# The order of one step's front work on TensorE: head sums and key norms last

## The chip, the core and the metric

The kernel runs on one NeuronCore of one Trainium2 chip, as a single launch. The metric is the device time of the launch in microseconds (us). The profile's engines are TensorE (PE, with its weight loads as PEld), VectorE (DVE), ScalarE (ACT), GpSimd (POOL) and SyncE (SP), which issues most of the DMAs. TensorE writes only to PSUM, which has eight banks of 128 partitions by 512 float32 numbers. One matmul result of this kernel fits in one bank.

## The reference, cut to what matters

The input is x, of shape (4, 1024, 128). The layer first normalises each row, and then runs a linear-attention recurrence with 16 heads of 8 channels each:

```
q, k, v = silu(x @ Wq), silu(x @ Wk), silu(x @ Wv)
f       = sigmoid(x @ Wf1 @ Wf2)                 # exp(log_sigmoid)
gamma   = -sigmoid(x @ Wg)                       # one per head
k       = k / max(norm(k per head), 1e-12)
a       = k * gamma
S1 = S + a (k . S);  S2 = f * S1;  S3 = S2 + a (k . S2) + k v;  o = q . S3
out3 = stack([0, 0, o]) ... out = out3[:, -N:]   # every third row carries an o
```

The result is gated, normalised again, projected with Wout and added to x. After it comes a mixture of experts: a router chooses one of 16 experts for each token, and a shared expert runs beside them. Only the o of the last third of the recurrence reaches the output, and in the output every third row (here called "mixed") has an attention part. The other two thirds (called "others") do not, so their part of the router can be worked out early.

## The kernel before, in words

**Tiling.** The 1024 tokens of each sequence are cut into 32 chunks (C = 32), so that 4 x 32 = 128 chunks lie on the partitions. The recurrence over time becomes the product of per-token 8 x 8 matrices. Each chunk builds the product of its own matrices and a running sum of its v terms, walking backward through its tokens. These are the backward loops. There are NT = 32 steps: steps 0 to 20 walk the first 21 slots of each chunk (L1 = 21), and steps 21 to 31 walk the last 11 (L2 = 11). After them a chain on VectorE joins the chunks, a forward loop follows, and then come the gate, the projection and the experts.

**One step of the backward loops.** It works on two halves h of the state, half 1 first, and each half lives in PSUM banks 2h and 2h + 1. `grow` (line 1531) multiplies the state by three factors in one VectorE instruction. TensorE's `sums(h, i)` (lines 1952 and 1953) adds over heads: line 1952 gives what `u_term` (line 1553) needs, and line 1953 gives what `y_term` (line 1559) needs. `next_state` (line 1565) adds the terms and waits for GpSimd's `add_u_term` (line 1131). VectorE's order in loop pass i is: u_term and y_term of half 1, u_term of half 0, next state of half 1, y_term of half 0, grow of half 1 for step i, next state of half 0, grow of half 0, and then `front(i)`. ScalarE's `ucopy` (line 926), GpSimd's `v_times_u` (line 1045) and TensorE's `add_sum` (line 1962) gather the v terms.

**The front work.** Each step also carries some preparation for later steps. A group of 3 or 4 slots is transposed (kind `xT`, line 1745), projected (`K`, `V`, `Q`, `G`, `F`, line 1757), its key norms are worked out (`squares`, line 1765; `rk`, line 1774), and a head sum is formed (`c`, line 1779). Work for the gate (`xaT`, line 1796; `gate`, line 1802), for the router of the "others" rows (`rowsT`, line 1810; `logits`, line 1820; `ranks` and `totals`, line 1828) and the transposes of two weights (`ffn_w`, line 1786) is spread over the steps too. The function `uses(i)` lists the items of step i. It is the one source of their order, and all four engines walk that list.

**Banks.** All front items share banks 6 and 7. `ports()` deals the banks out strictly by turns: item number k over all steps gets bank 6 + k % 2. TensorE's `port(kind, n)` waits until the item before on the same bank has been taken, and then fills the bank. ScalarE takes most items: `evict` (line 776), `evict_slot` (line 783), and line 846 for `totals`. VectorE takes two kinds: `rk` in `keys` (line 1468) and `c` in `c_keys` (line 1475). VectorE does this in its `front(i)`, which walks `uses(i - 1)`, the list of the step before, and stands behind both grow instructions of step i. The same `front` runs the router's parts from step 22 on: part 4, in step 26, is the scan at line 1310, and it first waits until `totals` has been taken.

**TensorE's order** in step i is sums of half 1 and half 0 (each waits for its grow), add_sum of both halves for step i - 1, and then `front(i)`. Its queue is in order, so a front item that waits holds back the sums of step i + 1. GpSimd's `y_keys` feeds `c`; it runs in the same step, and its next call waits until the `c` before has been filled. No engine writes an order by cost: all of it is written out by hand.

Of the kernel before, what the change touches and what calls it, by code (L numbers as in the profile page):

```python
# [127 lines left out]

def uses(i):

    found = []
    if i == 0:
        found += [("K", 2), ("V", 2)]
    if i == 1:
        found += [("G", 2), ("F", 2)]
    for n in range(EARLY, NG):
        ahead = NEED[n] - i
        if ahead == 8:
            found.append(("xT", n))
        if ahead == 7:  # L140
            found += [("K", n), ("V", n)]
            if GROUPS[n][0] >= L1:
                found.append(("Q", n))
        if ahead == 6:
            found += [("G", n), ("F", n)]
    for n in range(2, NG):
        ahead = NEED[n] - i
        if ahead == 5:
            found.append(("squares", n))
        if ahead == 4:  # L150
            found.append(("rk", n))
        if ahead == 2:
            found.append(("c", n))
    if i in (2, 3):
        found.append(("ffn_w", i - 2))
    for g in range(NQ):
        if i == 8 + 4 * g:
            found.append(("xaT", g))
        if i == 11 + 4 * g:
            found.append(("gate", g))  # L160
    for g in range(len(OTHERS.groups)):
        if i == 9 + 2 * g:
            found.append(("rowsT", g))
        if i == 10 + 2 * g:
            found.append(("logits", g))
    if i == 25:
        found += [("ranks", 0), ("totals", 0)]
    return found


FIRST = [("xT", 0, 0), ("K", 0, 2), ("low", 0, 7), ("xT", 1, 1), ("K", 1, 3), ("wfo", 0, 7), ("squares", 0, 6),
# [4 lines left out]
def ports():  # L176

    count, at = [0] * 8, {}

    def put(kind, n, b):  # L180
        at[kind, n] = (b, count[b])
        count[b] += 1

    for kind, n, b in FIRST:
        put(kind, n, b)
    first = list(count)
    for k, (kind, n) in enumerate(u for i in range(NT) for u in uses(i)):
        put(kind, n, 6 + k % 2)
    return at, first, count
# [9 lines left out]
def build(nc, a, out, xs, ys, scr):  # L199

    ctx = ExitStack()
    with ctx:
# [526 lines left out]
        def _(act):  # L729
# [76 lines left out]
            def front(i):  # L806

                for kind, n in uses(i):
                    if kind == "xT":
                        evict(kind, n, xnT[n % 2][:, 0:wide_of(n)], cols=wide_of(n))  # L810
# [105 lines left out]
            for i in range(NT):  # L916
                for kind, n in uses(i):
                    if kind == "rk":
                        spread_rk(n)
                if i == L1:  # L920
                    copy_sums(b_out.rearrange("p (a b) -> p a b", a=2))
                for h in (1, 0):

                    act.wait_ge(s_uterm[h], i + 1)
                    act.wait_ge(s_bp[h], i + 1)
                    S.activation(ucopy[:, h], bank[2 * h + 1], ACT.Copy).then_inc(s_uc[h], 1)  # L926
                front(i)
# [1236 lines left out]
```

## Time and profile before

| what | value |
|---|---|
| median of 3 runs | 642.89 us (642.54 to 643.53) |
| profiled execution | 641.85 us, its span 639.7 us, mean granted clock 0.947 |
| PE busy | 522.9 us (82%) |
| DVE busy | 493.5 us (77%) |
| POOL busy | 382.3 us (60%) |
| ACT busy | 252.4 us (39%) |
| chain that ended last | PE 34%, DVE 31%, issue 16%, POOL 13% |
| grow, L1531 | 64 instructions, 112.2 us, 1753 ns each |

How to read it: the span is the time between the first and the last event of the profiled execution. "Idle before" is the time an engine stood still just before an instruction, with the instruction that released it. In a timeline, each line is one instruction (or several of one kind, merged) with its start, its duration and that idle time in brackets. TensorE runs a float32 matmul as two passes, which show as x2. The end of a matmul is modelled, so the starts of the next ones are the safer reading. The granted clock is 1.00 at 2.4 GHz and 0.50 at 1.2 GHz.

### The profile page before, as it was taken

Reading aid. Unit: us, or ns where it says so; the run is one execution under the profiler, and the core shown is the slowest. Engines: PE = TensorE matmul, PEld = TensorE weight load, DVE = VectorE, ACT = ScalarE, POOL = GpSimd, SP = SyncE. Lnnn points to the kernel's source line nnn. Section 1 sums busy time; section 2 is a strip of 40 time slices with the busy share of each in tenths; the row PEclk is TensorE's granted clock in tenths of the full one; section 3 lists DMA queues with packets and bytes.
Section 4 is the critical chain, followed back from the end, with each engine's and each line's share of the span. In section 5 each row is a group of like instructions: output and inputs, shape, how many; then the busy total and the mean of one; then the engine's idle time right before and its main releaser. Section 6 shows DMA issues by size and latency. Waiting matters only on the chain.

```text
span 639.7 us, 7393 instructions
## 1 busy us (share of the span) xinstructions
PE 522.9 (82%) x1809; PEld 273.2 (43%) x1810; DVE 493.5 (77%) x799; ACT 252.4 (39%) x530; POOL 382.3 (60%) x394
## 2 busy tenths in 40 slices
PE   3889898989999886966786789889999967766883
PEld 2543434444444333322454455434544255434551
DVE  5697999989898999799899998688999773413331
ACT  4476543444444332110533344525455115121341
POOL 2378776757576465654776233476676575674553
PEclk9999999999999998898999799989999975976997
DMA  6801137900000691000521123200000011123440
GB/s 171 202 19 33 33 85 215 232 1 1 1 1 1 165 341 53 2 0 0 153 70 49 35 83 90 50 17 25 25 25 17 1 50 41 37 79 93 116 105 9
DMA packets 49572, 43.57 MB, mean 68 GB/s; under 512 B 5160, under 2 KB 42790, under 8 KB 49160
## 3 DMA queue, kind: packets, MB, share of 16 engines
q1 hardware_dynamic: 45220, 36.67, 21.6%
q0 software_dynamic: 3280, 6.09, 3.4%
q10 hardware_dynamic: 1040, 0.43, 0.2%
q8 instruction: 13, 0.21, 0.1%
q14 instruction: 19, 0.16, 0.1%
HBM read 24.80 MB, written 19.37 MB: 69 GB/s over the span
## 4 chain that ended last, share of the span: by engine, by line
PE 34%; DVE 31%; issue 16%; POOL 13%; ACT 3%; DMA 2%; SPq 1%; POOLq 0%; DVEq 0%; ACTq 0%
DVE grown L1531 10%; PE ps L1999 8%; PE ps L2016 5%; POOL grown L1131 5%; DVE ps L1565 4%; PE ps L1952 3%; DVE early L1637 3%; PE ps L2006 2%; PE ps L2056 2%; POOL uv L1045 2%; DVE early L1632 2%; DVE grown L1553 2%; PE ps L1757 2%; POOL slot_rows L1060 2%; PE ps L2057 2%
## 5 line engine op out<-in xcount | busy, mean ns | idle before, releaser
L1131 POOL TENSOR_TENSOR grown<-grown 128x512 f32<-128x512 f32 x64 | 80.5, 1268 | 91.7 <-DVE grown L1553 91.7
L1531 DVE TENSOR_TENSOR grown<-ps,steps 128x1536 f32<-128x1536 f32 x64 | 112.2, 1753 | 1.6
L1952 PE MATMUL ps<-grown,cst 128*128 128x512 f32 x128 | 72.8, 652 | 24.6 <-DVE grown L1531 24.2
L926 ACT ACTIVATE uv<-ps 128x512 f32<-128x512 f32 x64 | 38.1, 597 | 104.8 <-DVE grown L1553 104.8
L1999 PE MATMUL ps<-steps 128*128 x128 | 70.1, 646 | 8.2 <-issue 8.2
L1045 POOL TENSOR_TENSOR uv<-uv,steps 128x512 f32<-128x512 f32 x64 | 67.5, 1076 | 1.6 <-ACT uv L926 1.6
L1953 PE MATMUL ps<-grown,cst 128*128 128x512 f32 x128 | 68.0, 614 | 0.0
L1962 PE MATMUL ps<-uv,cst 128*128 128x512 f32 x128 | 60.4, 594 | 1.1 <-POOL uv L1045 1.1
L1423 DVE TENSOR_TENSOR e_h<-rk,ps 128x256 f32<-128x256 f32 x64 | 25.2, 417 | 42.7 <-ACT rk L943 29.4
L1207 POOL TENSOR_TENSOR early<-state,qT 128x512 f32 x22 | 37.1, 1688 | 34.0 <-DVE state L1545 34.0
L1553 DVE TENSOR_TENSOR grown<-ps,steps 128x512 f32<-128x512 f32 x64 | 43.3, 677 | 7.6 <-PE ps L1952 7.6
L1565 DVE TENSOR_TENSOR ps<-ps,grown 128x512 f32<-128x512 f32 x60 | 41.6, 694 | 9.4 <-POOL grown L1131 9.4
L1637 DVE TENSOR_REDUCE early<-early 128x32 f32<-128x288 f32 x63 | 42.6, 676 | 4.3 <-POOL early L1178 2.2
L1952 PEld LDWEIGHTS ps<-grown,cst 128*128 128x128 f32 x128 | 21.4, 197 | 56.7 <-DVE grown L1531 49.9
L1559 DVE TENSOR_TENSOR ps<-ps,steps 128x512 f32<-128x512 f32 x64 | 44.2, 690 | 1.8 <-PE ps L1953 1.8
L943 ACT ACTIVATE rk<-ps 128x256 f32<-128x256 f32 x64 | 23.9, 383 | 52.6 <-PE ps L1999 51.0
L1237 POOL DMA_INDIRECT out<-e_y,e_to x26 | 26.2, 1008 | 27.0 <-DVE e_y L1709 22.6
L1178 POOL COPY early<-early 128x32 f32<-128x32 f32 x63 | 19.3, 307 | 34.4 <-DVE early L1637 34.2
L2016 PE MATMUL ps<-steps,e_hT 128*128 x256 | 37.2, 290 | 2.7 <-ACT e_hT L947 2.7
L1953 PEld LDWEIGHTS ps<-grown,cst 128*128 128x128 f32 x128 | 25.2, 197 | 32.5 <-issue 32.5
L1962 PEld LDWEIGHTS ps<-uv,cst 128*128 128x128 f32 x128 | 24.2, 190 | 32.4 <-issue 29.7
L2016 PEld LDWEIGHTS ps<-steps,e_hT 128*128 128x128 f32 x256 | 32.7, 197 | 9.1 <-issue 8.0
(233 smaller groups left out, 1022.8 us busy)
## 6 DMA issues: line engine op xcount, KB each, us to landing
steps<-gate_up_proj SPq DMA_DIRECT2D x1, 4096.0 KB, 16.1
xs_others<-zeros SPq DMA_DIRECT2D x1, 2496.0 KB, 10.8
steps<-xs_others SPq DMA_DIRECT2D x19, 128.0 KB, 2.1
ys_others<-e_y SPq DMA_DIRECT2D x19, 128.0 KB, 1.8
early<-chain_m SPq DMA_DIRECT2D x4, 512.0 KB, 6.2
xf<-x SPq DMA_DIRECT2D x4, 495.0 KB
normed<-early SPq DMA_DIRECT2D x28, 64.0 KB, 1.7
slot_rows<-no_row SPq DMA_DIRECT2D x1, 1741.5 KB, 13.9
```

What stands on the lines that cost most here:

```text
L1045: return G.tensor_tensor(wide(dst, w), wide(src, w), per_col(tile, k, 1, h, w), ALU.mult)
L1131: G.tensor_tensor(decayed[:, h], decayed[:, h], work[:, h, 1], ALU.add).then_inc(s_add[h], 1)
L1531: V.tensor_tensor(grown[:, :, h].rearrange("p e (x w) -> p e x w", w=HD), st, per_col(tile, FF, 3, h, HD), ALU.mult).then_inc(s_prod[h], 1)
L1553: V.tensor_tensor(wide(work[:, h, 1], HD), wide(ps[h][:, 1], HD), per_col(tile_of(i), PP, 1, h, HD), ALU.mult).then_inc(s_uterm[h], 1)
L1559: V.tensor_tensor(wide(bank[2 * h], HD), wide(bank[2 * h], HD), per_col(tile_of(i), K, 1, h, HD), ALU.mult).then_inc(s_term[h], 1)
L1565: V.tensor_tensor(dst, bank[2 * h], decayed[:, h], ALU.add).then_inc(s_state[h], 1)
L1637: V.tensor_reduce(ch_s[:, :, i + 1, :].rearrange("p i v -> p v i"), ch_pr[:, m % 2].rearrange("p v j i -> p v i j"), AX.X, ALU.add).then_i ...
L1952: T.matmul(bank[2 * h + 1], c["block"], work[:, h, 1], start=True, stop=True).then_inc(s_usum[h], 1)
L1953: T.matmul(bank[2 * h], c["minus"], work[:, h, 0], start=True, stop=True).then_inc(s_red[h], 1)
L1962: T.matmul(bank[4 + h], c["ident"], vterm[:, h], start=i in (0, L1), stop=i + 1 in (L1, NT)).then_inc(s_ba[h], 1)
L1999: T.matmul(b_gu(run, b)[u], e_xT[:, b, u], gu[:, bass.ds(ex * (2 * F), 2 * F)], start=True, stop=True).then_inc(s_eg, 1)
L2016: ins = T.matmul(b_y(run)[:, u * D:(u + 1) * D], e_hT[:, u, f * P:(f + 1) * P], dw[:, bass.ds(ex[u] * F + f * D, D)], start=(f == 0), stop ...
```

## The change

Within each step, `uses(i)` now puts the items that VectorE takes (`rk` and `c`) behind all the others. The items of a step stay the same, and so does their number, so the steps before and after keep their banks unless the order inside them changes.

```diff
 def uses(i):
 
-    found = []
+    found, late = [], []
     if i == 0:
         found += [("K", 2), ("V", 2)]
...
         if ahead == 5:
             found.append(("squares", n))
         if ahead == 4:
-            found.append(("rk", n))
+            late.append(("rk", n))
         if ahead == 2:
-            found.append(("c", n))
+            late.append(("c", n))
...
     if i == 25:
         found += [("ranks", 0), ("totals", 0)]
-    return found
+    return found + late
```

Worked out from `uses` and `ports`, the lists differ in eight of the 32 steps (item, group @ bank):

```
step  before                                   after
 3    G3@6 F3@7 c2@6 ffn_w1@7                  G3@6 F3@7 ffn_w1@6 c2@7
 9    xT5@6 rk4@7 rowsT0@6                     xT5@6 rowsT0@7 rk4@6
11    G5@6 F5@7 c4@6 gate0@7 rowsT1@6          G5@6 F5@7 gate0@6 rowsT1@7 c4@6
13    xT6@6 rk5@7 rowsT2@6                     xT6@6 rowsT2@7 rk5@6
15    G6@7 F6@6 c5@7 gate1@6 rowsT3@7          G6@7 F6@6 gate1@7 rowsT3@6 c5@7
17    xT7@7 rk6@6 rowsT4@7                     xT7@7 rowsT4@6 rk6@7
19    G7@6 F7@7 c6@6 gate2@7 rowsT5@6          G7@6 F7@7 gate2@6 rowsT5@7 c6@6
25    rk8@6 ranks0@7 totals0@6                 ranks0@6 totals0@7 rk8@6
```

## Rows read from the trace of the kernel before

**Rows 1.** Busy time per engine, backward loops: us, busy (x), then PEclk, DMA share, GB/s

```profile
48.00:303.00 255.00, 221.72 (x624) 101.41 (x623) 230.98 (x284) 101.53 (x167) 168.16 (x146) 0.97 0.27 73
```

**Rows 2.** Who VectorE waited for in the loops: total us, times, longest

```profile
DVE grown L1553 <- PE ps L1952: 7.6, 12, 1.7
```

**Rows 3.** Timeline of PE, step 11's front, then step 12's sums

```profile
126.57 1.02 PE L1757 MATMUL ps<-e_hT,wge 128*128 128x512 f32 x2
127.42 1.02 PE L1757 MATMUL ps<-e_hT,wfo 128*128 128x512 f32 x2
128.37 1.10 PE L1779 MATMUL ps<-e_y,cst 128*128 128x512 f32 x2
129.30 1.02 PE L1802 MATMUL ps<-gateT,wfo 128*128 128x512 f32 x2
131.92 0.63 PE L1810 MATMUL ps<-cst,early 128*128 128x128 f32 x4 [1.60 <-DVE steps L1475]
132.39 1.02 PE L1952 MATMUL ps<-grown,cst 128*128 128x512 f32 x2
```

**Rows 4.** Timeline of DVE: a step without a stall, then step 12

```profile
115.49 0.68 DVE L1553 TENSOR_TENSOR grown<-ps,steps 128x512 f32<-128x512 f32 x1
...
118.83 1.75 DVE L1531 TENSOR_TENSOR grown<-ps,steps 128x1536 f32<-128x1536 f32 x1
...
131.10 0.68 DVE L1475 TENSOR_TENSOR steps<-steps,ps 128x512 f32<-128x512 f32 x1
133.45 0.69 DVE L1553 TENSOR_TENSOR grown<-ps,steps 128x512 f32<-128x512 f32 x1 [1.67 <-PE ps L1952]
```

**Rows 5.** Timeline of ACT: it takes G, F and gate of step 11

```profile
127.62 0.60 ACT L783 ACTIVATE steps<-ps 128x512 f32<-128x512 f32 x1 [0.81 <-PE ps L1757]
128.48 0.60 ACT L783 ACTIVATE steps<-ps 128x512 f32<-128x512 f32 x1 [0.26 <-PE ps L1757]
130.36 0.60 ACT L776 ACTIVATE gateT<-ps 128x512 f32<-128x512 f32 x1 [1.28 <-PE ps L1802]
```

**Rows 6.** Timeline of PE: G of step 15, then step 16's sums

```profile
161.88 1.02 PE L1757 MATMUL ps<-e_h,wge 128*128 128x512 f32 x2
...
166.66 1.02 PE L1952 MATMUL ps<-grown,cst 128*128 128x512 f32 x2
```

**Rows 7.** Timeline of PE: G of step 19, then step 20's sums

```profile
196.15 1.02 PE L1757 MATMUL ps<-e_hT,wge 128*128 128x512 f32 x2
...
200.71 1.02 PE L1952 MATMUL ps<-grown,cst 128*128 128x512 f32 x2
```

**Rows 8.** Timeline of ACT: it takes gate of step 19

```profile
199.73 0.49 ACT L776 ACTIVATE gateT<-ps 128x384 f32<-128x384 f32 x1 [1.06 <-PE ps L1802]
```

**Rows 9.** Timeline of PE, step 25's front: rk, ranks, totals

```profile
250.37 0.83 PE L1774 MATMUL ps<-cst,early 128*128 128x128 f32 x6
251.03 0.76 PE L1828 MATMUL ps<-early,cst 128*128 128x352 f32 x2
255.36 1.51 PE L1828 MATMUL ps<-early,cst 128*128 128x352 f32 x2 [3.57 <-DVE steps L1468]
```

**Rows 10.** Timeline of DVE, step 26 up to step 27's grow

```profile
254.67 0.54 DVE L1468 TENSOR_TENSOR steps<-steps,ps 128x384 f32<-128x384 f32 x1
257.40 0.89 DVE L1310 TENSOR_TENSOR_SCAN early<-early 128x352 f32<-128x352 f32 x1 [2.19 <-ACT early L846]
...
263.34 1.75 DVE L1531 TENSOR_TENSOR grown<-ps,steps 128x1536 f32<-128x1536 f32 x1
```

**Rows 11.** Timeline of ACT: it takes ranks of step 25

```profile
251.83 0.46 ACT L776 ACTIVATE early<-ps 128x352 f32<-128x352 f32 x1 [2.05 <-PE ps L1828]
```

**Rows 12.** Timeline of PE: step 10's sums, behind the rk front of step 9

```profile
112.64 1.12 PE L1952 MATMUL ps<-grown,cst 128*128 128x512 f32 x2
```

**Rows 13.** Busy time per engine and PEclk at step 26's stall (columns as in Rows 1)

```profile
254.00:256.00 2.00, 0.64 (x1) 0.50 (x2) 1.21 (x2) 0.00 (x0) 0.00 (x0) 0.51 0.00 0
256.00:258.00 2.00, 2.00 (x4) 1.01 (x3) 0.60 (x1) 0.46 (x1) 0.00 (x0) 0.50 0.04 8
```

**Rows 14.** Busy time per engine and PEclk in the experts of mixed rows

```profile
560.00:600.00 40.00, 27.41 (x102) 16.55 (x103) 10.06 (x19) 9.92 (x24) 22.13 (x27) 0.79 0.33 92
```

## The prediction

> **What bounds the kernel now.** I read the busy time by stretch first. In the backward loops VectorE is busy for 230.98 of 255.00 us [rows 1], so it sets the pace and only its idle time can be won. The view of waits comes next: its u_term waited for TensorE's sums 12 times, 7.6 us in total [rows 2]. The timelines of steps 12 to 27 show where. The three longest stalls, at steps 12, 16 and 20, have one shape. In TensorE's front, rowsT is on the same bank as c, two places behind it. VectorE takes c only behind both of its grows of the next step, so TensorE stands 1.60 us [rows 3] and the next sums start late. Step 26 is the fourth case: totals is on the bank of rk, TensorE stands 3.57 us [rows 9], and VectorE itself then waits 2.19 us for ScalarE to take totals [rows 10]. VectorE waits for a result that can't come before its own earlier instruction. In this kernel that is a bubble in the engine that sets the pace.
>
> **Which steps change.** The change reorders steps 3, 9, 11, 13, 15, 17, 19 and 25. It adds no instruction and no bytes and moves no DMA; SP's and POOL's queues keep their order. ScalarE takes neither rk nor c, so its own order and its table loads stay as they are too. Each step keeps its item count, so no other step changes banks; only whose taking the first item of the next step waits for changes, and there the item has been taken well before.
>
> **Step 11 (head sum c4).** Three lags come from rows. ScalarE takes G 1.05 us after TensorE started it (126.57 to 127.62), needs 0.60, and TensorE starts the next user of the bank 0.15 us later (128.22 to 128.37) [rows 3, 5]. After the change:
> - G and F start at 126.57 and 127.42, as now.
> - gate is on G's bank and starts at 128.37, where c starts now.
> - rowsT is on F's bank. F has been taken at 129.08, and gate needs its 0.93 us (129.30 - 128.37), so rowsT starts at 129.30. It holds TensorE for 0.47 (131.92 to 132.39), until 129.77.
> - c is now on gate's bank. ScalarE takes gate 1.06 after its start (129.30 to 130.36), at 129.43, until 130.03, and c starts at 130.18. This is the wait that the change adds, 0.4 us on TensorE. The sums of step 12 are queued behind it.
> - c needs 0.87, so the sums start at 131.05 instead of 132.39.
>
> VectorE wants c at 131.10 [rows 4] and gets it about 1.06 after its start, at 131.24, and u_term starts 1.06 after its sums (132.39 to 133.45): at 132.11 instead of 133.45. The gain is 1.34 us. The other end: if c needed no wait, u_term would start when VectorE is free, at 131.70, and the pace behind it would be the undisturbed one (115.49 to 118.83, 3.34 us from u_term to grow [rows 4]) instead of 3.52. That would be 1.94 us. At the low end, c held until VectorE's own c_keys is merely late, I put 0.9. I take 1.34, since every link of it has a row.
>
> **Steps 15 and 19 (c5, c6).** Here TensorE enters the front later against VectorE. G starts at 161.88, which is 35.31 after step 11's [rows 6], and the same sequence puts the sums at 131.05 + 35.31 = 166.36 instead of 166.66: 0.30 us. In step 19 the shift is 69.58 [rows 7]. gate has 384 columns there, so it is taken 0.21 earlier in the sequence (199.73 - 69.58 = 130.15 against 130.36) and in 0.49 instead of 0.60 [rows 8]. The sums start at 131.05 + 69.58 - 0.32 = 200.31 instead of 200.71: 0.40 us. Bounds for each: from 0 (ScalarE's taking of gate takes the place of VectorE's, fully) to 1.9 and 1.7 (as in step 11, with no new wait).
>
> **Step 25 (rk8, ranks, totals).** ranks starts at 250.37 and needs 0.65. ScalarE takes it 0.80 after its start (251.03 to 251.83), for 0.46 [rows 9, 11]: from 251.17 to 251.63. totals is on the other bank, starts at 251.02, and is taken by 252.3. rk8 waits for ranks, starts at 251.78 and needs 0.66, which ends at 252.44. Step 26's grow of half 1 ends at 252.35, so the sums are late by 0.1 at most. VectorE starts keys at 254.67 and then the scan at once, at 255.13 instead of 257.40 [rows 10]. u_term starts 0.82 behind it at 255.95, and the next grow 3.34 later, at 259.29 instead of 263.34. The gain is 4.05 us. It needs no link whose row is missing. Its low end is 2.3 (the wait of the scan alone goes); its high end is 4.1.
>
> **Steps 3, 9, 13, 17.** In step 3 no two items of one bank stand with c between them, and there was no stall. In steps 9, 13 and 17 rk now waits for ScalarE to take xT. By the lags above this delays the next sums by some 0.35 to 0.5 us. The cover is VectorE's own work: in step 10 the sums started at 112.64 [rows 12], u_term could have gone at 113.70, and it went at 115.49 [rows 4], so 1.8 us are spare. keys gets its bank more than 1 us before VectorE comes to it. I take 0; without that cover it would be up to 1.4 us in all.
>
> **The sum.** 1.34 + 0.30 + 0.40 + 4.05 = 6.1 us. All that follows the loops waits for their state, and the weight DMAs issued at step 21 have landed long before they are needed, so I pass it on one for one. The profiled execution took 641.85 us (span 639.7, 2.1 around it) and would take 635.8. The median is 642.89, 1.04 above it, and becomes 636.8.
>
> **The clock.** In the stall of step 26 the granted clock falls to 0.51 and stays at 0.50 in the next 2 us [rows 13], which is the 1.2 GHz level, after TensorE had stood for 3.57 us [rows 9]. The stall's loss in my sum already holds that. After the change this stretch has work, but step 26 has no front items: TensorE will be through with it at some 258.4 (my estimate, sums and add_sum of 0.9 us a half from 254.8 on) and stand until step 27's grow ends at 259.29 + 1.75 = 261.04, 2.6 us. A fall there would make one sum of 0.87 us twice as long on the path, up to 0.8 us. The Trainium skill (TensorE: Matmul & The Clock Gate, the section on why this matters for your kernels) says to leave no long idle gap between bursts of matmuls, or the clock goes back to half rate. By that rule the removal of the stall keeps the clock, and 4.05 stands; the rule agrees with the trace in step 26. If the gap before step 27 counts as long too, the sum is 5.3.
>
> **Rivals.**
> - *The gap moves to step 27.* The clock falls there: 642.89 - 5.3 = 637.6. For: a fall already costs matmuls double in this loop. Against: the gap is shorter than the one that brought the fall. 12%.
> - *Only step 25 gains.* In steps 11, 15 and 19 the new wait on ScalarE for gate, or VectorE's wait for a late c, takes the place of the old one. 642.89 - 4.05 = 638.8. For: in steps 15 and 19 nearly all of it goes that way in my own sum. Against: the eviction in step 11 has every link in rows. 15%.
> - *All stalls go.* If c starts without a wait: 1.94 + 1.9 + 1.7 + 4.05 = 9.6, which gives 633.3. Against: gate can't be taken before it is made. 6%.
> - *No effect.* c and rk last make VectorE wait in each of the eight steps by what TensorE gains, or the loop's gain is taken back by a wait that I don't see: 642.9. Against: rows 9 and 10 show the stall of step 25 with both ends. 3%.
> - *Slower: the tail loses the clock.* In the experts of the mixed rows the granted clock is 0.79 [rows 14]. An earlier start shifts TensorE's gaps against what grants the clock. It decides from 6.1 us of matmul time lost, that is 12.2 us more at half clock on the path; 16 us more would give 642.89 - 6.1 + 8 = 644.8. Against: the engines' order and gaps in that stage don't change. 4%.
>
> The forecast itself, 636.8, has 60%.
>
> **Range and chances.** A difference of 0.2% (1.3 us) is about what a measurement of this kernel can tell from no change. The forecast with its own spread is 635.8 to 637.8. The range takes in the clock rival and the one in which only step 25 gains, but not the one in which all stalls go: 634.8 to 639.2. Faster 0.93 (the forecast and the three rivals that keep step 25), same 0.03, slower 0.04.
>
> **What would show it.** In the new trace rowsT (L1810) of steps 11, 15 and 19 has no wait for VectorE L1475, and c (L1779) stands behind it with an idle of some 0.4 us for ScalarE's gate. u_term's wait at step 12 shrinks from 1.67 to about 0.3, and those at steps 16 and 20 shrink by 0.3 and 0.4 only. The wait of 3.57 us at L1828 and the scan's 2.19 us are gone, and from step 26's grow to step 27's it is about 8.7 us instead of 12.7. It is wrong if VectorE shows new waits at L1475 or L1468 of over 0.5 us, if the 12.7 us stay, or if the loops end 6 us earlier and the whole doesn't.

## The result and the profile after

The changed kernel takes 635.67 us (median of 4 runs, 632.82 to 636.75) where the kernel before takes 642.71 (4 runs, 640.96 to 643.53). The ratio is 0.9887, with a 95% interval of 0.9849 to 0.9926: 1.1% faster, and clear of no change. Two later comparisons, each with 11 or 12 runs of the changed kernel, give 0.9936 (0.9910 to 0.9962) and 0.9937 (0.9910 to 0.9964). The forecast of 636.8 stands 1.1 us above the first median. The later ratios put the gain at 4.1 us, so the whole-kernel times say 4 to 7 us, and the traces have to say the rest.

The profiled execution took 635.28 us with a span of 633.1 (before: 641.85 and 639.7). The busy times hardly moved, as nothing was added or removed: this is page part 1 of the changed kernel.

```profile
PE 519.4 (82%) x1809; PEld 270.6 (43%) x1810; DVE 494.1 (78%) x799; ACT 251.6 (40%) x530; POOL 382.3 (60%) x394
```

The main reading is the distance from one step's grow of half 1 to the next one's, taken from the starts of L1531 in VectorE's timeline. Of the 31 distances, 26 agree between the two traces to 0.02 us. The five others are:

```
grow of step      before    changed   difference
12 to 13            9.94       8.71        -1.23
16 to 17            9.93       9.76        -0.17
20 to 21           10.43      10.16        -0.27
26 to 27           12.74       8.65        -4.09
27 to 28            8.39       9.04        +0.65
sum                                        -5.11
```

TensorE's timeline of step 11's front, and VectorE's of step 12, answer to [rows 3, 4]:

```profile
128.23 1.10 PE L1802 MATMUL ps<-gateT,wfo 128*128 128x512 f32 x2
129.17 0.60 PE L1810 MATMUL ps<-cst,early 128*128 128x128 f32 x4
130.11 1.10 PE L1779 MATMUL ps<-e_y,cst 128*128 128x512 f32 x2 [0.34 <-ACT gateT L776]
131.04 1.02 PE L1952 MATMUL ps<-grown,cst 128*128 128x512 f32 x2
```

```profile
131.24 0.69 DVE L1475 TENSOR_TENSOR steps<-steps,ps 128x512 f32<-128x512 f32 x1 [0.20 <-PE ps L1779]
132.10 0.69 DVE L1553 TENSOR_TENSOR grown<-ps,steps 128x512 f32<-128x512 f32 x1 [0.17 <-PE ps L1952]
```

rowsT (L1810) has no wait for VectorE any more. c (L1779) now waits 0.34 us for ScalarE's taking of gate, and that bubble is all that the new order costs there. This trace began 0.12 us earlier than the one before at the same point; with that taken off, the sums come 1.23 us earlier.

Behind the front of step 15, VectorE's wait has moved more than it has shrunk. This is VectorE in the changed kernel, and then its u_term in the kernel before:

```profile
165.34 0.69 DVE L1475 TENSOR_TENSOR steps<-steps,ps 128x512 f32<-128x512 f32 x1 [1.24 <-PE ps L1779]
166.19 0.69 DVE L1553 TENSOR_TENSOR grown<-ps,steps 128x512 f32<-128x512 f32 x1 [0.17 <-PE ps L1952]
```

```profile
167.72 0.69 DVE L1553 TENSOR_TENSOR grown<-ps,steps 128x512 f32<-128x512 f32 x1 [1.67 <-PE ps L1952]
```

Before, L1475 had no wait there. TensorE runs c right in front of the sums now, so VectorE waits at c for what it used to wait for at u_term, and the sums come only 0.17 us earlier.

Steps 25 and 26 answer to [rows 9, 10]. First TensorE, then VectorE:

```profile
247.62 1.35 PE L1828 MATMUL ps<-early,cst 128*128 128x352 f32 x4
249.02 0.91 PE L1774 MATMUL ps<-cst,early 128*128 128x128 f32 x6
250.61 1.13 PE L1952 MATMUL ps<-grown,cst 128*128 128x512 f32 x2 [0.68 <-DVE grown L1531]
```

```profile
252.87 0.54 DVE L1468 TENSOR_TENSOR steps<-steps,ps 128x384 f32<-128x384 f32 x1
253.33 0.88 DVE L1310 TENSOR_TENSOR_SCAN early<-early 128x352 f32<-128x352 f32 x1
254.13 0.67 DVE L1553 TENSOR_TENSOR grown<-ps,steps 128x512 f32<-128x512 f32 x1
```

The 3.57 us hold at L1828, the scan's 2.19 us and u_term's wait are gone, and TensorE now waits for VectorE's grow. VectorE has no wait for TensorE left in step 26.

The loss in front of step 28 is a single instruction, the router's L1313, which runs beside GpSimd's y_keys (L1103). The timelines of GpSimd and VectorE, in the changed kernel and then in the one before:

```profile
261.29 1.00 POOL L1103 TENSOR_TENSOR e_y<-steps 128x384 f32<-128x384 f32 x1
...
261.52 1.16 DVE L1313 TENSOR_TENSOR early<-cst,early 128x352 f32<-128x352 f32 x1
```

```profile
266.55 0.99 POOL L1103 TENSOR_TENSOR e_y<-steps 128x384 f32<-128x384 f32 x1
...
267.40 0.52 DVE L1313 TENSOR_TENSOR early<-cst,early 128x352 f32<-128x352 f32 x1
```

### The profile page after: what moved, and what is told of

The parts are those of the page before. It is cut to its first block, busy times and chain, and to the rows that moved or that the text cites. A ratio compares the mean times of both kernels' runs of the same rounds, so it can differ in the third digit from the quotient of the medians.

```text
span 633.1 us, 7393 instructions
## 1 busy us (share of the span) xinstructions
PE 519.4 (82%) x1809; PEld 270.6 (43%) x1810; DVE 494.1 (78%) x799; ACT 251.6 (40%) x530; POOL 382.3 (60%) x394
## 4 chain that ended last, share of the span: by engine, by line
PE 42%; DVE 25%; issue 14%; POOL 12%; ACT 3%; DMA 2%; SPq 1%; POOLq 0%; DVEq 0%; ACTq 0%
PE ps L1999 8%; DVE grown L1531 7%; PE ps L2016 5%; PE ps L1952 4%; POOL grown L1131 4%; PE ps L1953 3%; PE ps L1962 3%; DVE ps L1565 3%; PE ps L1757 3%; DVE early L1637 3%; PE ps L2006 2%; DVE early L1632 2%; PE ps L2056 2%; POOL uv L1045 2%; POOL slot_rows L1060 2%
## 5 line engine op out<-in xcount | busy, mean ns | idle before, releaser
L1531 DVE TENSOR_TENSOR grown<-ps,steps 128x1536 f32<-128x1536 f32 x64 | 112.1, 1752 | 1.6
L1952 PE MATMUL ps<-grown,cst 128*128 128x512 f32 x128 | 71.6, 642 | 27.2 <-DVE grown L1531 26.8
L1999 PE MATMUL ps<-steps 128*128 x128 | 71.6, 659 | 8.5 <-issue 8.5
L1045 POOL TENSOR_TENSOR uv<-uv,steps 128x512 f32<-128x512 f32 x64 | 67.5, 1077 | 1.6 <-ACT uv L926 1.6
L1953 PE MATMUL ps<-grown,cst 128*128 128x512 f32 x128 | 67.0, 606 | 0.0
L1565 DVE TENSOR_TENSOR ps<-ps,grown 128x512 f32<-128x512 f32 x60 | 41.6, 693 | 9.7 <-POOL grown L1131 9.7
L1637 DVE TENSOR_REDUCE early<-early 128x32 f32<-128x288 f32 x63 | 42.6, 677 | 4.3 <-POOL early L1178 2.2
L1237 POOL DMA_INDIRECT out<-e_y,e_to x26 | 27.5, 1059 | 27.5 <-DVE e_y L1709 23.1
```

The lines of the kernel that those rows point to most:

```text
L1045: return G.tensor_tensor(wide(dst, w), wide(src, w), per_col(tile, k, 1, h, w), ALU.mult)
L1531: V.tensor_tensor(grown[:, :, h].rearrange("p e (x w) -> p e x w", w=HD), st, per_col(tile, FF, 3, h, HD), ALU.mult).then_inc(s_prod[h], 1)
L1565: V.tensor_tensor(dst, bank[2 * h], decayed[:, h], ALU.add).then_inc(s_state[h], 1)
L1637: V.tensor_reduce(ch_s[:, :, i + 1, :].rearrange("p i v -> p v i"), ch_pr[:, m % 2].rearrange("p v j i -> p v i j"), AX.X, ALU.add).then_i ...
L1952: T.matmul(bank[2 * h + 1], c["block"], work[:, h, 1], start=True, stop=True).then_inc(s_usum[h], 1)
L1953: T.matmul(bank[2 * h], c["minus"], work[:, h, 0], start=True, stop=True).then_inc(s_red[h], 1)
```

## The experiments

They are labelled e1 to e12, and each stands beside the kernel before on its chip. The runs lay on three chips, and the kernel before took 656.0, 642.1 and 656.7 us there. That difference lies behind the loops: where a kernel leaves a step alone, the step's distance is the same on all three chips to 0.03 us (only the one from step 0 to 1, still in the input stage, varies). So the distances decide, and the ratios stand beside them. A distance is named by the later of its two grows: "13" is from step 12 to 13, and the front of step 11 bears on it; the front of step 12 bears on 14.

**One step alone (e1).**

```diff
-            late.append(("rk", n))
+            (late if i == 25 else found).append(("rk", n))
-            late.append(("c", n))
+            found.append(("c", n))
```

> The kernel before, with rk last in step 25 alone. Theory (TensorE's queue is held by an item whose bank VectorE has not freed, and the stall is the sum of such holds): steps 12, 16 and 20 keep their u_term waits of 1.67, 1.67 and 1.45 us; in step 25 the 3.57 us at L1828 and the scan's 2.19 us are gone, and step 26's grow to step 27's takes 8.65 us instead of 12.74. Whole: 4.1 us less, 638.6. Rival (the gain of the whole change comes from VectorE's two kinds being last in every step, by less contention or a better granted clock): well under 4 us from this one step, 640 to 642.

Measured: ratio 0.9949 (0.9920 to 0.9979). The distances in front of steps 13, 17 and 21 are those of before (9.94, 9.93, 10.44), step 27's is 8.65 and step 28's is 9.02. So this one step brings 4.09 us and loses 0.63 in the next. The theory holds, by the distances: the ratio's interval alone would leave room for the rival.

**The head sums alone (e2).** `(late if i in (11, 15, 19) else found).append(("c", n))`, with rk as before.

> The kernel before, with c last in steps 11, 15 and 19 alone. Theory: u_term of steps 12, 16 and 20 starts 1.2, 0.2 and 0.3 us earlier (as in the changed kernel's trace), step 26 keeps its 12.7 us. Whole: 1.7 us less, 641.0, at the edge of what can be told. Rival (the wait for ScalarE's taking of gate replaces the hold): 0 to 0.3 us less in the loops.

Measured: ratio 0.9969 (0.9943 to 0.9995). The distances are 8.72, 9.76 and 10.16, so 1.66 us together, as expected. The 12.7 us of step 26 did not stay: they became 11.68, although nothing in that step was changed. The granted clock goes with it. The stall ends 1.99 us earlier in this trace (TensorE's `totals` starts at 253.37 instead of 255.36), so 256 to 258 here stands beside 258 to 260 of the kernel before. First the busy view of this kernel, then that of the one before:

```profile
256.00:258.00 2.00, 2.00 (x5) 0.84 (x4) 1.35 (x3) 0.60 (x1) 0.60 (x1) 0.80 0.00 0
```

```profile
258.00:260.00 2.00, 2.00 (x3) 0.67 (x2) 0.99 (x2) 0.60 (x1) 0.62 (x1) 0.50 0.00 0
```

The granted clock is back at 2.4 GHz within this stretch (0.80 on its mean), where before it stayed at 0.50. VectorE's wait at the scan is the same, 2.19 us. TensorE's own idle time was longer here, 4.51 us instead of 3.57, and yet the stretch at 1.2 GHz behind it was shorter. No run changes the clock alone.

**The other four steps (e3).** `(late if i in (9, 13, 17) else found)` for rk and `(late if i == 3 else found)` for c.

> The kernel before, with rk last in steps 9, 13 and 17 and c last in step 3: the four steps that I put at nothing. Theory: TensorE starts the next sums 0.3 to 0.5 us later in steps 10, 14 and 18, VectorE's 1.8 us of own work cover it, and every grow starts within 0.1 us of the kernel before: 0.0 us, 642.7. Rival (moving rk late costs): up to 0.5 us in each of three steps, 1.4 us more, 644.1.

Measured: ratio 0.9986 (0.9959 to 1.0013), and every distance from step 2's to step 26's is that of before within 0.02 us; step 27's is 0.10 longer. The new wait is there, and it is covered; this is TensorE's timeline of step 9's front:

```profile
112.25 1.13 PE L1774 MATMUL ps<-cst,early 128*128 128x128 f32 x8 [0.34 <-ACT e_hT L776]
113.22 1.02 PE L1952 MATMUL ps<-grown,cst 128*128 128x512 f32 x2
```

Against the grow of half 1, the sums start 0.24 us later than before (2.05 us behind its start instead of 1.81), and not 0.35 to 0.5. The theory holds: these four edits are worth nothing.

**The hold or the scan's wait (e4).**

```diff
-        found += [("ranks", 0), ("totals", 0)]
+        found += [("totals", 0), ("ranks", 0)]
```

> The kernel before, with totals and ranks exchanged in step 25 (rk8, totals, ranks): totals no longer shares rk8's bank, so the scan has its input early, but ranks now does, so TensorE is held as long as before. Theory (what counts is TensorE's hold, since the sums of step 26 stand behind it): the scan's wait of 2.19 us goes, u_term waits about 2.2 us longer in its place, and step 26's grow to step 27's takes 12.3 to 12.8 us: 0 to 0.4 us less in all, 642.5. Rival (the scan's own wait is what costs): 2.2 us less, 640.5.

Measured: ratio 1.0005 (0.9980 to 1.0031), distance 13.05. The scan no longer waits, and all of it comes back at u_term, as VectorE's timeline shows:

```profile
255.77 0.88 DVE L1310 TENSOR_TENSOR_SCAN early<-early 128x352 f32<-128x352 f32 x1
259.26 0.69 DVE L1553 TENSOR_TENSOR grown<-ps,steps 128x512 f32<-128x512 f32 x1 [2.60 <-PE ps L1952]
```

The longest wait in VectorE's own list of that step was not the price. TensorE's queue was. The distance is even 0.3 us longer than before, and there my expectation was too low. By the granted clock in stretches of 1 us, it was back at 1.00 at 262.2, 6.2 us behind the start of the matmul that ends the stall, and before at 260.9, 5.5 us behind it. The second u_term of the step waits 0.84 us instead of 0.52.

**The changed kernel again**, on the second (e5) and the third chip (e12).

> The changed kernel once more, beside the kernel before on this chip. Theory: the loops' 32 grows stand apart as in its first trace to 0.05 us (8.71, 9.76, 10.16 and 8.65 us in front of steps 13, 17, 21 and 27), whatever the chip does behind the loops, and the whole is 5 us less than before. Rival (part of the 7 us of the first comparison was the change itself in a later stage): more than 6 us less again.

Measured: ratio 0.9936 (0.9910 to 0.9962), and all distances from step 1 on as in the first trace to 0.02 us. The theory holds: what the first comparison showed over 5 us did not come back. The intervals of e5 and e12 reach to 5.8 and 5.9 us less, so they take in the 5.1 us of the loops and not the 6.1 us of my sum.

> The changed kernel beside the three kernels above, for their comparison on one chip: 5 us (0.8%) less than the kernel before, with the same 32 grow distances as in its two traces.

Measured: ratio 0.9937 (0.9910 to 0.9964), with the same distances to 0.02 us.

**An order in which no item should wait (e6)**, in steps 11, 15 and 19 of the changed kernel:

```diff
+    if i in (11, 15, 19):
+        first = {"rowsT": 0, "G": 1, "F": 2, "c": 3, "gate": 4}
+        return sorted(found + late, key=lambda u: first[u[0]])
     return found + late
```

> The changed kernel with steps 11, 15 and 19 in the order rowsT, G, F, c, gate: c stands behind F and its bank is G's, gate is last. Theory (TensorE's bubble in front of c is ScalarE's taking of gate, 0.3 us, and no item has to wait in this order): the sums behind these fronts start 0.35 to 0.45 us earlier, VectorE no longer waits for c (2.7 us of waits at L1475 go to nearly 0 but u_term waits in their place), and the grows of steps 13, 17 and 21 come 0.4, 0.4 and 0.35 us earlier: 1.2 us less than the changed kernel. Rival (VectorE's wait for c is itself the price, 0.2, 1.24 and 0.92 us): 2.3 us less.

Measured: ratio 0.9950 (0.9924 to 0.9975). The distances are 9.20, 10.23 and 10.30 instead of 8.71, 9.76 and 10.16: 1.1 us slower, not 1.2 faster. Both readings of mine were wrong. ScalarE's timeline of step 11 shows why (line numbers are 3 higher in this kernel):

```profile
128.07 0.60 ACT L779 ACTIVATE wnat<-ps 128x512 f32<-128x512 f32 x1 [1.69 <-PE ps L1813]
128.68 1.28 ACT L786 ACT_TABLE_LOAD   x1
129.98 1.08 ACT L786 ACTIVATE steps<-ps 128x512 f32<-128x512 f32 x2
```

The load of the Sigmoid table stands in front of the first Sigmoid item. With G first, it ran while ScalarE was idle (from 125.40, with the first Sigmoid at 127.49, in the changed kernel). With rowsT, a plain copy, first, it runs after that copy, G's bank comes free late, and c waits 0.81 us for it instead of 0.34 for gate's. In steps 15 and 19 it is 0.81 and 0.76 us. VectorE's waits at L1475 shrank to 0, 0.84 and 0.41 us, and the steps took longer all the same.

**Gate one step later (e7)**: `if i == 12 + 4 * g` in place of `if i == 11 + 4 * g`.

> The changed kernel with each gate item one step later (steps 12, 16, 20), so that 0.9 us of TensorE work leaves the fronts of steps 11, 15 and 19. Theory (what is left there is plain TensorE work in front of the sums): step 13's grow comes 0.7 us earlier, step 17's 1.0 and step 21's 0.8 to 0.9, and the fronts of steps 12, 16 and 20 hold it for nothing: 2.5 us less than the changed kernel. Rival (the work only moves, and steps 13, 17 and 21 start late instead): less than 1 us.

Measured: ratio 0.9943 (0.9919 to 0.9968). Distances 13, 17 and 21 shrink by 0.72, 1.02 and 0.70, as expected. But 14 and 18 grow by 1.01 and 1.30, and 16 and 20 by 0.32 each: 0.5 us slower in sum. The rival was right: the fronts of steps 12 and 16 have no 0.9 us to spare. The front of step 20 has: distance 22 stays at 8.83.

**Q one step earlier (e8)**: Q is appended at `NEED[n] - i == 8`, behind xT and rowsT and in front of rk.

> The changed kernel with each Q item one step earlier (steps 13, 17, 21, in front of rk). Theory: TensorE's lateness in steps 15 and 19 comes from the fronts of steps 14 and 18 (three projections and logits), and it is what makes c5 and c6 1.0 us later than c4. The u_term waits of 0.57 us in steps 15 and 19 go, grow of step 17 comes 1.0 us and that of step 21 0.9 us earlier: 2.0 us less than the changed kernel. Rival (steps 15 and 19 are bound by their own fronts): 0.1 us less.

Measured: ratio 0.9917 (0.9890 to 0.9944). u_term's waits of 0.57 us in steps 15 and 19 are gone, and distances 17 and 21 shrink by 0.56 and 0.55: about half of what I expected. VectorE's waits at L1475 in steps 16 and 20 fell from 1.24 and 0.92 to 0.68 and 0.36 us, where step 12 has 0.19: Q in the fronts of steps 14 and 18 is 0.56 us of TensorE's lateness, and not all of it. Distances 15 and 19 stay at 8.00, so the fronts of steps 13 and 17 have room for the extra item; 23 grows by 0.15.

**Gate behind rk, two steps later (e9).**

```diff
-        if i == 11 + 4 * g:
-            found.append(("gate", g))
+        if i == 13 + 4 * g:
+            late.append(("gate", g))
```

> The changed kernel with each gate item two steps later, in steps 13, 17 and 21, behind rk. Theory (the fronts with G, F, c and rowsT are too long for TensorE by the gate's 0.9 us, while the fronts with xT, rowsT and rk have over 1 us to spare): the grows of steps 13, 17 and 21 come 0.7, 1.0 and 0.7 us earlier, as with gate one step later, and the steps behind 13, 17 and 21 take no longer (8.10 us), where gate one step later cost 1.0 and 1.3 us: 2.4 us less than the changed kernel. Rival (any front that gets the gate pays it): less than 0.5 us.

Measured: ratio 0.9889 (0.9858 to 0.9920), beside 0.9937 for the changed kernel on this chip. Distances 13, 17 and 21 shrink by 0.71, 1.02 and 0.71; 14, 15, 18 and 19 stay. 16 and 20 grow by 0.32 and 0.57, which I had not expected, so it is 1.6 us instead of 2.4. The traces of e9 and e12 show where from: against grow, the sums behind the fronts of steps 13 and 17 start 0.6 and 0.85 us later. The steps themselves cover that, but the three projections of steps 14 and 18 still start 0.3 and 0.6 us later, and u_term's waits in steps 15 and 19 grow from 0.56 to 0.89 and 1.14 us. The room in front of one step was partly the room of the step after it.

**GpSimd's two zeroings one pass later each (e10)**: `if i in (2, 4, 5)` in place of `if i in (2, 3, 4)`, with the slices moved along, on top of e9.

> As the kernel with gate behind rk, and GpSimd's two zeroings of the rows for the router stand in its passes 4 and 5 instead of 3 and 4, away from the pass that also forms the products of group 2. Theory (the wait of 2.15 us for GpSimd in step 4 is that one zeroing of 1.27 us in front of its add): step 4's grow comes 1.2 to 1.4 us earlier (9.41 us become 8.0 to 8.2), and the later zeroing costs nothing: 3.7 us less than the changed kernel. Rival (the two steps after it pay instead, or the rows for the router arrive late in step 8): 2.4 us less or under it.

Measured: ratio 0.9874 (0.9842 to 0.9906), median 647.83 beside 652.77 of the changed kernel. Distance 4 falls from 9.42 to 8.21 and 6 rises by 0.16, so the zeroings bring 1.05 us where I expected 1.2 to 1.4. By the distances this kernel is 2.6 us faster than the changed kernel, and not 3.7; the rest of what is missing is e9's. It is the fastest of all. In the kernel before, VectorE's waits for GpSimd at L1565 were 9.2 us in the loops (23 times), more than u_term's 7.6 us for TensorE, and the change leaves them alone.

**Q earlier as well, on top of e10 (e11).**

> As the kernel before it, with Q in steps 13, 17 and 21 too, in front of rk. Theory (each of these fronts has some 1.3 us to spare, which gate has used by 0.9): steps 14 and 18 now wait 0.3 to 0.6 us for the sums, and steps 17 and 21 gain up to 0.7 each: within 0.5 us of the kernel without it. Rival (the spare time is larger): 1.4 us less than it.

Measured: ratio 0.9936 (0.9906 to 0.9965). Against the kernel without it, distances 15, 19 and 23 grow by 0.99, 1.23 and 2.12 us, and 16 and 20 shrink by 0.52 and 0.76. With the smaller differences it is 2.65 us slower in sum, so theory and rival were both wrong. The room in the rk fronts is good for one item and not for two.

## Why the prediction was right

- **What bounds the kernel: right, but not in every step.** All of the difference in the loops is idle time of VectorE or one instruction of it that ran longer. In steps 12, 16 and 20 VectorE then waits for plain TensorE work: taking gate out of those fronts shortens them by 0.7 to 1.0 us more (e7, e9).
- **The four steps and no others: right.** E1 to e3 split the change into parts that add up: 4.09, 1.66 and 0.00 us in the distances that I had named. Step 26's own distance also moved by -1.06 us in e2 and +0.10 in e3, with the clock.
- **Step 11: 1.34 forecast, 1.23 measured.** Every link was there, but the wait stood elsewhere: I left 1.4 and 1.05 us of it at u_term in steps 16 and 20, and it is 0.17 us there in all three steps, with 0.20, 1.24 and 0.92 us at L1475. ScalarE takes gate 1.14 us after its start (128.23 to 129.37) and not 1.06, and c holds TensorE for 0.93 (130.11 to 131.04) and not 0.87. Those two lags, 0.14 us together, are also about the whole of the error in steps 15 (0.30 against 0.17) and 19 (0.40 against 0.27).
- **The wait that the change adds: right.** ScalarE's taking of gate takes the place of VectorE's taking of c, as my sum had it in steps 15 and 19. The sign I gave for error, new waits of over 0.5 us at L1475, did show (1.24 and 0.92), and it was a bad sign: such a wait costs nothing while the sums behind it come later still. In e6 those waits were shorter in sum and the steps longer.
- **Step 25: 4.05 forecast, 4.09 measured.** I had the mechanism and the size. The sums are 0.16 us behind grow's end in e1 (252.43 to 252.59), where I had put 0.1 at most; in the changed kernel TensorE was earlier still and waited 0.68 us for grow. My sentence that the row of the stall holds the clock's part was right as well, but that part isn't fixed: the stall cost 3.03 (e2), 4.09 (before), 4.19 (e3) and 4.40 us (e4) over the 8.65 of the kernel without it.
- **The cover of rk: right**, with e3 for it.
- **Passed on one for one: not quite.** I left out what VectorE's earlier start runs into. L1313 now stands beside y_keys and takes 1.16 us instead of 0.52; that and the overlap lost around it is 0.65 us. So the loops give 5.1 us, where my sum said 6.1. (From the first grow to the chain's first reduction, L1637, it is 284.86 against 280.12, 4.7 us; 0.15 of the rest is the first L1632, 1.17 us instead of 1.02, again an SBUF-only instruction beside GpSimd.) That the first comparison stands near the forecast is good luck: 1.7 us of its two traces' difference in span lie behind the chain's first reduction, where I had forecast nothing, and the two later comparisons agree with 5.
- **The rival of the clock in step 27: its gap came, its price did not.** TensorE stood 2.55 us there, where I had estimated 2.6. In the changed kernel the clock stayed at 1.00; in e1 it fell, and TensorE's block sums took 2.07 us, but VectorE had no wait in that step, since L1313 held it just as long (9.02 against 9.04). The Trainium skill (TensorE: Matmul & The Clock Gate, the section on why this matters for your kernels) warns of long idle gaps; the fall at the 3.57 us stall agrees with it, but it doesn't tell the two traces with the same 2.55 us apart. My argument against this rival, that the gap is shorter than the one that brought the fall, was weak: the kernel before had already fallen to 0.50 from 243.8 on, behind an idle time of 1.75 us.
- **What stays open:** from the chain's first reduction to the end of the span, the traces take 325.7 to 332.5 us where the kernel before takes 642 us, and 342.0 to 349.0 where it takes 656, without an order by kernel. I haven't looked for its cause.

## What to carry to other kernels

Where several engines empty a small set of PSUM banks by turns, look for an item whose bank is freed by the engine that is itself waiting for the filler's next result; put it last in its group. (Letting another engine free it is the other way; no run here tried it.) Price it at the queue that is held, not at the wait that looks longest: a wait removed elsewhere comes back in front of the same matmul. Then check each front for room one item at a time, look two steps on for lateness that is passed along, and keep an item that needs a new activation table first, where its load falls into idle time.

## What the runs showed of the hardware

**L1313 ends a fixed time behind GpSimd's y_keys.** L1313 has both of its inputs in SBUF, and y_keys works in SBUF too. In all 14 traces L1313 started before y_keys had ended, and it ended 0.37 to 0.39 us behind y_keys: y_keys ended at 262.29, 264.16 (e1) and 264.82 (e2) and L1313 at 262.68, 264.55 and 265.20, with durations of 1.16, 1.16 and 0.83 us. In the kernel before, e3 and e4 it started only 0.13 or 0.14 us before y_keys' end, and took 0.52. The first L1632, also with SBUF inputs only, does the same behind GpSimd's L1045: it ends 0.29 and 0.28 us behind it (before and changed) and takes 1.02 and 1.17 us, where the ones after it take 0.42 or 0.43. The 64 instructions of L1531, which read PSUM and often run beside GpSimd, all took 1746 to 1758 ns in the kernel before. That is a reading of traces; no run here isolates it. The Trainium skill (SBUF — State Buffer, the section on SBUF's two separate sides) says that the two engines share a port pair, which a VectorE instruction with two SBUF inputs or a GpSimd instruction takes for the whole of its time while the other waits; the traces agree.

**ScalarE's table load is 1.28 us, and its place in the order counts.** In e6 it stands between the first copy and the first Sigmoid, TensorE waits 0.81, 0.81 and 0.76 us instead of 0.34, 0.34 and 0.29 for a bank, and the three steps take 1.1 us more. No run moves the load alone.

**The same idle time can leave TensorE's clock at 2.4 GHz or take it to 1.2.** After 2.55 us of idle in front of step 27's sums it stayed at 1.00 in the changed kernel and was at 0.50 in e1, whose order of work in that step is the same. In front of step 25's sums TensorE stood 1.75 us in six traces: the clock then fell to 0.50 in the kernel before, in e1, e3 and e4, and stayed at 1.00 in the changed kernel and in e2. Distance 26 is 8.98 to 9.00 us either way, so that fall cost nothing.
